# A Mamba-2 layer between two expert layers, one core: weight loads, VectorE's state updates and ScalarE's gated copies in another order

## The reference, cut to what matters

```python
proj = hidden_states @ W_in.T               # z, xBC, dt
xBC = silu(causal_conv(xBC, conv_w, K=4) + conv_b)   # x, B, C
dt = softplus(dt + dt_bias)
Y_diag = einsum('bclhn,bcshn,bhcls,bcshp->bclhp', C_c, B_c, Lmat, x_dt)   # Lmat: decays inside a chunk
states = einsum('bclhn,bhcl,bclhp->bchpn', B_c, decay_states, x_dt)
new = prev * exp(d_k)[..., None, None] + s_k          # the state, chunk after chunk
Y_off = einsum('bclhn,bhcpn,bhcl->bclhp', C_c, prev_states, exp(A_cum))
y = Y_diag + Y_off + D_param * x
g = y * silu(z)
out = (g * rsqrt(mean(g * g) + EPS) * norm_w) @ W_out.T
```

## Time and profile before

| | |
|---|---|
| median of 3 runs | 2531.59 us (2530.6 to 2532.52) |
| profiled execution, its own time | 2530.1 us |
| span of the profiled execution | 2528.3 us |
| TensorE busy | 2290.8 us, 91% of the span |
| VectorE busy | 1742.7 us, 69% |
| GpSimd busy | 1475.2 us, 58% |
| ScalarE busy | 1408.7 us, 56% |

### The profile page before, as it was taken

How to read it: one execution, slowest core, us unless ns; L and a number is a source line. 1 busy time by engine, 2 the same in 40 slices (tenths; PEclk the granted TensorE clock), 3 DMA queues, 4 the chain that set the end, 5 groups by cost and what they waited for, 6 DMA issues and landing times. The chain is left out here.

```text
span 2528.3 us, 44164 instructions
## 1 busy us (share of the span) xinstructions
PE 2290.8 (91%) x11910; PEld 1785.7 (71%) x11910; DVE 1742.7 (69%) x3592; ACT 1408.7 (56%) x2859; POOL 1475.2 (58%) x1306
## 2 busy tenths in 40 slices
PE   4899976999999999999878999999999998489997
PEld 2687755777777777777656777777777776268776
DVE  6532275678787888777867878787878787753225
ACT  3133324677667766776536767677766675323332
POOL 1876341666666666666416666666666665178533
PEclk8999988999999999999889999999999999689998
DMA  8665441333333334333203434443343331166545
GB/s 316 235 184 165 139 135 34 100 88 87 95 103 88 87 95 97 94 87 87 73 10 99 103 88 86 95 102 87 87 95 104 87 87 50 50 224 184 164 151 170
DMA packets 204905, 285.32 MB, mean 113 GB/s; under 512 B 16289, under 2 KB 148459, under 8 KB 204817
## 3 DMA queue, kind: packets, MB, share of 16 engines
q1 hardware_dynamic: 185936, 219.18, 32.4%
q0 software_dynamic: 18880, 65.02, 8.3%
HBM read 225.43 MB, written 58.72 MB: 112 GB/s over the span
## 5 line engine op out<-in xcount | busy, mean ns | idle before, releaser
L1289 POOL TENSOR_TENSOR mamba_mix<-mamba_mix,mamba_scores 128x512 f32<-128x512 f32 x256 | 330.5, 1291 | 278.9 <-ACT mamba_mix L1473 278.9
L1951 PE MATMUL mamba_p_proj<-mamba_xt_lo,mamba_in_hi 128*128 128x512 f32 x1056 | 464.3, 440 | 20.5 <-DVE mamba_bc L1662 11.6
L1952 PE MATMUL mamba_p_proj<-mamba_xt_hi,mamba_in_hi 128*128 128x512 f32 x1056 | 417.1, 395 | 0.0
L1953 PE MATMUL mamba_p_proj<-mamba_xt_hi,mamba_in_lo 128*128 128x512 f32 x1056 | 416.8, 395 | 0.0
L1469 ACT ACTIVATE mamba_mix<-mamba_cum_l,mamba_cum_g 128x128 f32<-128x128 f32 x1024 | 324.5, 390 | 0.0
L1657 DVE SCALAR_TENSOR_TENSOR mamba_xs<-mamba_p_proj,mamba_taps,mamba_xs 128x511 f32<-128x511 f32 (+2 forms) x384 | 285.4, 743 | 40.8 <-ACT mamba_xs L1403 31.7
L1283 POOL TENSOR_TENSOR mamba_xend<-mamba_xdt,mamba_to_end_g 128x512 f32<-128x512 f32 x128 | 160.4, 1253 | 213.7 <-DVE mamba_xdt L1715 213.7
L1688 DVE TENSOR_TENSOR mamba_total<-mamba_p_out,mamba_total 128x512 f32<-128x512 f32 x256 | 176.9, 691 | 149.0 <-PE mamba_p_out L1987 144.4
L643 DVE TENSOR_TENSOR ffn_h<-ffn_p_gu,ffn_sil 128x256 f32<-128x256 f32 x110 | 46.7, 425 | 304.4 <-ACT ffn_sil L532 304.1
L1951 PEld LDWEIGHTS mamba_p_proj<-mamba_xt_lo,mamba_in_hi 128*128 128x128 f32 x1056 | 202.3, 192 | 75.3 <-DVE mamba_bc L1662 12.3
L1953 PEld LDWEIGHTS mamba_p_proj<-mamba_xt_hi,mamba_in_lo 128*128 128x128 f32 x1056 | 200.6, 190 | 45.0
(11 more groups left out here) (334 smaller groups left out, 5465.2 us busy)
## 6 DMA issues: line engine op xcount, KB each, us to landing
mamba_cum_l<-mamba_cum_rows SPq DMA_DIRECT2D x128, 512.0 KB, 6.0
mamba_rise<-mamba_exp_rows SPq DMA_DIRECT2D x256, 128.0 KB, 5.6
ffn_xs<-slots_in SPq DMA_DIRECT2D x78, 256.0 KB, 2.7
slots_out<-ffn_y SPq DMA_DIRECT2D x78, 256.0 KB, 2.3
mamba_raw_x<-in_t SPq DMA_DIRECT2D x34, 512.0 KB, 7.3
mamba_raw_z<-in_t SPq DMA_DIRECT2D x32, 512.0 KB, 8.0
mamba_raw_out<-out_t SPq DMA_DIRECT2D x32, 512.0 KB, 3.7
slots_out<-ffn_xs SPq DMA_DIRECT2D x1, 9984.0 KB, 42.0
```

Source lines behind the costliest of these rows:

```text
L1289: pool.tensor_tensor(mix[:, c % 2, :, :], mix[:, c % 2, :, :], scores[:, b * CPB + c, :].unsqueeze(1).broadcast_to([P, GH, P]), ALU.mult). ...
L1951: pe.matmul(bank, in_hi[:, piece, kk, :], xt_lo[:, kk, c], start=(kk == 0), stop=False)
L1952: pe.matmul(bank, in_hi[:, piece, kk, :], xt_hi[:, kk, c], start=False, stop=False)
L1953: last = pe.matmul(bank, in_lo[:, piece, kk, :], xt_hi[:, kk, c], start=False, stop=(kk == KT - 1))
```

## The change

SyncE: `load_in` for the next group moves ahead of `load_out`, of the decays of half a slot and of their exponentials; the loop now runs from group 2, with group 1's round written ahead of it, and the last three loads follow the loop. ScalarE: `high` of tile 1 moves behind `tap_x` of tile 0. VectorE: `combine` is split in `carry_state` (carried part and state) and `add_skip`; at the start of a slot carry_state(0) stands between the two gating products and add_skip(0) behind them, and combine(1) now precedes add_carry(0). From chunk 2 on `carry_state` has a wait for the sum of two chunks before. No instruction of arithmetic or transfer is added or removed.

```diff
--- before.py
+++ after.py
@@ -1202,20 +1202,29 @@
                     load_cum(k, 0, 0, j, first=True)
                 for j in range(2):
                     load_rise(k, 0, 0, j, first=True)
-                load_cum(k, 0, 1, 0)
-                with sp.Fori(1, G) as gi:
+
+                def round_of(gi, second=False):
                     load_in(gi + (sx + 1), gi * GC + X0, gi * 4 + (sz + 2), gi * GC + Z0)
+                    if not second:
+                        load_out(gi + (k * G - 1), gi - 1)
+                    load_cum(k, gi, -1, 0)
+                    if not second:
+                        load_rise(k, gi, -2, 1)
                     load_cum(k, gi, -1, 1)
                     load_rise(k, gi, -1, 0)
                     load_cum(k, gi, 0, 0)
                     load_rise(k, gi, -1, 1)
                     load_cum(k, gi, 0, 1)
                     load_rise(k, gi, 0, 0)
-                    load_out(gi + k * G, gi)
-                    load_cum(k, gi, 1, 0)
-                    load_rise(k, gi, 0, 1)
+
+                round_of(1, second=True)
+                with sp.Fori(2, G) as gi:
+                    round_of(gi)
                 if k + 1 < batches:
                     load_in(sx + G + 1, B0, sz + 4 * G + 2, DT0, HEADS)
+                load_out(k * G + G - 1, G - 1)
+                load_cum(k, G - 1, 1, 0)
+                load_rise(k, G - 1, 0, 1)
                 load_cum(k, G - 1, 1, 1)
                 for j in range(2):
                     load_rise(k, G - 1, 1, j)
@@ -1511,10 +1520,11 @@
                     for i in range(NB):
                         lns.root(act, k + 1, i)
                 if not first:
-                    for ct in range(CT):
-                        high(U - 1, gp, 1 - b, ct, second)
+                    high(U - 1, gp, 1 - b, 0, second)
                 if not last:
                     tap_x(k, gn, bn, 0, first)
+                if not first:
+                    high(U - 1, gp, 1 - b, 1, second)
                 exponents(k, gi, b, 2)
                 if not first:
                     for ct in range(CT):
@@ -1667,11 +1677,11 @@
                 for i in steps:
                     conv_step(k, gi, b, ct, gi * CT + ct, xs[:, b, ct, :], i)
 
-            def gate(k, gi, b):
+            def gate(k, gi, b, tiles=range(CT)):
 
                 U, V = unit(k, gi, b)
                 dve.wait_ge(s_sum, U * CPB + CPB)
-                for ct in range(CT):
+                for ct in tiles:
                     dve.wait_ge(s_zs, U * CT + ct + 1)
                     dve.tensor_tensor(zs[:, b, ct, :], xs[:, b, ct, :], zs[:, b, ct, :], ALU.mult).then_inc(s_g, 1)
 
@@ -1724,10 +1734,11 @@
                 gn, bn = (gi, 1) if b == 0 else (gi + 1, 0)
                 gp, bp = (gi, 0) if b == 1 else (gi - 1, 1)
 
-                def combine(c):
+                def carry_state(c):
 
                     n = U * CPB + c
-                    cols = slice(c * P, (c + 1) * P)
+                    if c >= 2:
+                        dve.wait_ge(s_sum, n - 1)
                     dve.wait_ge(s_y2, n + 1)
                     if c % 2 == 0:
                         dve.wait_ge(s_rise[c // 2], U * 32 + 32)
@@ -1737,11 +1748,19 @@
                     dve.wait_ge(s_decayed, n + 1)
                     dve.tensor_tensor(state[:, :, :], p_st[:, 0:GC].rearrange("p (h d) -> p h d", h=GH),
                                       decayed[:, :, :], ALU.add).then_inc(s_state, 1)
+
+                def add_skip(c):
+
+                    cols = slice(c * P, (c + 1) * P)
                     for ct in range(CT):
                         done = dve.scalar_tensor_tensor(xs[:, b, ct, cols], xs[:, b, ct, cols],
                                                         skip[:, bass.ds(gi * CT + ct, 1)], p_y[:, c % 2, 0, ct, :],
                                                         ALU.mult, ALU.add)
                     done.then_inc(s_y, 1)
+
+                def combine(c):
+                    carry_state(c)
+                    add_skip(c)
 
                 def add_carry(c):
 
@@ -1778,8 +1797,11 @@
                 if more:
                     layer_norm_of(k + 1)
                 if not first:
-                    gate(k, gp, bp)
-                combine(0)
+                    gate(k, gp, bp, (0,))
+                carry_state(0)
+                if not first:
+                    gate(k, gp, bp, (1,))
+                add_skip(0)
                 if not first:
                     gate_low(U - 1, gp, 1 - b)
                 elif k > 0:
@@ -1787,8 +1809,8 @@
                 next_rows(0, 1)
                 conv(0, (1,))
                 next_stats(0)
+                combine(1)
                 add_carry(0)
-                combine(1)
                 conv(0, (2,))
                 conv(0, (3,))
                 add_carry(1)
```

## The result

The changed kernel is slower: 2569.88 us (median of 4 runs, 2568.17 to 2571.0) against 2531.45 (4 runs of the kernel before), a ratio of 1.0149 with a 95% interval of 1.0136 to 1.0162. The direction was forecast, the size was not: +38 us in place of +15, outside the range of 2518 to 2566. The profiled execution has its own time of 2570.66 us.

The account below looks back on a forecast made before the run. TensorE was taken to bound the groups through its waits between steps. A group: +0.9 us (b = 0) less 0.4 (b = 1), +0.5, times 30 is 15 us, giving 2547 us; range 2518 to 2566.

Parts of the forecast that it names:

- What bounds the kernel: In the groups TensorE bounds, natural pace 4.45 us between recurrences; only its standing still between steps can be won or lost.
- SyncE's part: Next group's x weights issued 13 us earlier, their 1.16 us wait gone; the transfers they are moved past cost nothing.
- ScalarE's part: In b = 0 the second high runs behind tap_x(0); exponents(2) 0.65 us late, recur(2) from 808.31 to 808.94.
- b = 1: Slots with b = 1: state of chunk 0 about 1.3 us earlier, mix(3) 0.65 later; 0.4 us won per slot.
- The step that failed: b = 0, tile 0: low_x(0) holds the last halo piece to 811.0; project_z(0) at 811.15 in place of 809.89.
- r2-r3: Recur(2) to recur(3) in slots with b = 0, forecast to stay at about 5.1 us.
- first rival: In b = 0 low_x(0) goes before tile 0's second halo piece: +0.9 us a group, 28 us, 2559; chance 0.25.
- its worse form: Should mix(3) also precede tile 0's last halo piece, that waits until 812.9: some 1 us a group more, 2585.
- r3-next: Recur(3) of b = 0 to the next slot: forecast 11.6 us, tile 1's last halo piece held by second sum of squares.
- The forecast sum: Per group +0.9 us in b = 0 less 0.4 in b = 1: +0.5, times 30 groups, 15 us.
- The rival that ended on the other side: Holds miss the halo pieces: b = 0 costs +0.1, b = 1 gives 0.4; 9 us faster, 2522; chance 0.15.

Follow-up runs that it names:

- experiment 1: Kernel before with SyncE's part alone: weights issued early, ScalarE's and VectorE's orders as before; ratio to the kernel before 1.0037.
- experiment 6: Kernel before with early weights alone, halo pieces reading their left input from PSUM (left neighbours' values wrong); ratio to the kernel before 0.9892.
- Experiment 4: Changed kernel with GpSimd's low_x(0) moved from in front of mix(3) to right ahead of low_x(1); ratio to the kernel before 1.019.
- experiment 2: Kernel before with ScalarE's part alone: second high behind the first tap, weights late, VectorE's order as before; ratio to the kernel before 1.0104.
- experiment 3: Kernel before with VectorE's part alone: carry_state(0) between the gating products, combine(1) ahead of add_carry(0) in all slots; ratio to the kernel before 1.0015.
- experiment 5: Changed kernel with halo pieces reading their left input from PSUM instead of SBUF (left neighbours' values wrong); ratio to the kernel before 0.9941.
- experiment 7: Kernel before with VectorE's part alone, combine(1) ahead of add_carry(0) only in slots with b = 1, weights late; ratio to the kernel before 0.987.

## Why the prediction was right in its direction and wrong in its size

- *What bounds the kernel* was read rightly: where it waits for nothing TensorE's pace is 4.42 to 4.47 us a step in every run, and all that moved in the groups is waits between its steps.
- *SyncE's part*: as forecast, the weights 12 us earlier (13 said), their wait gone, and the transfers behind them harmless. That an early low_x(0) would fall on the halo pieces was right, and experiments 1 and 6 show it: +0.34 us a group with the pieces held, -0.99 with them free, both against the kernel before.
- *ScalarE's part*: recur(2) late by 0.63 was forecast for b = 0, 0.61 measured; gate_low's wait of 2 us, 2.00 measured.
- *b = 1*: +0.4 won was forecast, 0.54 measured.
- *The step that failed* is the turn between VectorE and GpSimd in b = 0, low_x(0) "runs from about 809.7 to 811.0", and the second halo piece due at about 809.7. I let the piece go first. Both times were right to 0.2 us, their order was not. In the trace low_x(0) starts at 819.85, 10.07 us behind recur(0), and the piece at 820.00, 10.22 behind it, and it is held 0.94 us (1.14 less 0.20). That is the first rival's order, to which I gave 0.25; the last piece then went ahead of mix(3), so its worse form did not come. r2-r3 is 5.58 where the forecast had 5.1.
- *A second term was too small*, in the rival as well. For r3-next I had 11.6 and for the rival's whole slot +1.3; measured 11.82 and +1.61. The forecast had the second sum of squares catch the last piece of tile 1 by its end; it caught the middle one from its start, and held it 1.1 us (1.30 less 0.21). The rival's own times were also added up wrongly: 825.9 less 824.51 is 1.4, not 1.3, and 30 x 0.9 is 27, not 28. Experiment 4 shows that moving one instruction did not free this end: what was freed in tile 0 was held in tile 1.
- *A term was missing*: I multiplied by 30 groups and put nothing on the rest. 10 of the 40 us of the span lie outside the loop groups. The traces tell where 4.3 of them come from: the first groups of the two sequences take 104.4 us together in the kernel before and 108.7 in the changed one, and 104.2, 106.1 and 107.1 in experiments 1, 2 and 3, so ScalarE's part brings 1.7 there, VectorE's 2.7 and SyncE's nothing. The 1.8 us by which the first recurrence is late need not be the change's: in experiment 5, which differs from the changed kernel in the halo pieces alone, it starts at 442.8 us as in the kernel before (442.5). What carries the rest stays open.

The sum with the measured terms is 28 x 1.08 + 10 = 40 us on the span, 1.1 us a group where +0.5 was written. The forecast sum had 15 us; some 16 of the other 25 lie in the loop groups (0.5 a group in r2-r3, 0.2 in r3-next, 0.1 won in b = 1) and 10 outside them. A range whose top case was the first rival's 28 us should have carried those edges too.

The rival that ended on the other side, holds that do not fall on the halo pieces, is what experiment 5 makes of the kernel: its b = 0 is 0.16 us shorter than before (the rival said 0.1 longer), and the ratio of 0.9941 is 15 us, where the rival said 9. So both branches had the right sign, but not the sizes: this one is -0.70 us a group where -0.3 was written. The direction was forecast by either order of the two instructions, 0.15 us apart, so the wrong order did not touch it; it made the loss larger.

## What to carry to other kernels

When a change lets GpSimd start sooner or VectorE later, list which VectorE instructions with two SBUF inputs then meet a GpSimd instruction, down to the smallest: a piece of two columns costs as much as what it runs into. Undo a change of several parts by slot and engine before judging it: here VectorE's part, with its second half kept to the slots with b = 1, was worth -1.3% and the whole was +1.5%. And where two instructions stand within a tenth of a microsecond, price both orders and give neither the name of likeliest; the loop of the changed kernel repeats one order in all 28 groups, that of experiment 3 splits 23 to 5.

## What the runs showed of the hardware

A held halo piece ends with GpSimd's instruction to 0.02 us: 821.14 and 821.12, 826.49 and 826.47 in the changed kernel, 833.31 and 833.29 in experiment 1. Experiments 5 and 6 show that it takes two inputs in SBUF: with the left one in PSUM none of 91 and 92 pieces took more than 215 ns.

Who goes first turns within a few hundredths of a microsecond. In the changed kernel the piece at 825.19 begins 0.01 us before the record of the sum of squares and is held through all of it, while the one at 821.72, 0.19 before mix(3), runs free. Over the traces of the eleven kernels that read the halo from SBUF, all 66 pieces that begin 0.00 to 0.02 us before GpSimd's next record are held, none of the 97 that begin 0.05 to 0.2 before it, and one of the two in between.

It works both ways. mix(3) at 821.91 starts just behind a sum of carried parts that VectorE began at 821.85 (until 822.26), also with both inputs in SBUF, and takes 1.51 us where mix(2) at 817.85 takes 1.28.

A copy with one SBUF input can be held too, which I had not expected. In experiment 7 the copy of 32 columns at the group's turn (before mostly 168 ns) has a median of 1278 ns, since it now begins just behind the start of GpSimd's low part of the output weights: in one group the copy takes from 787.37 to 788.65 us, the low part from 787.31 to 788.61. The copy's line, first before, then in experiment 7:

```profile
L1703 DVE COPY mamba_exp_last_g<-mamba_exp_last x32: 160/168/1290, 434.5 to 2093.7; 128x32 f32 x28, 128x32 f32<-128x32 f32 x4
```

```profile
L1703 DVE COPY mamba_exp_last_g<-mamba_exp_last x32: 169/1278/1292, 435.9 to 2065.0; 128x32 f32 x28, 128x32 f32<-128x32 f32 x4
```

It cost nothing there, since VectorE then still waits 0.86 us for TensorE's transposes. The Trainium skill, "SBUF — State Buffer", section "SBUF: two separate sides", counts VectorE's instructions in a 2-port mode among those that take the shared ports; the trace agrees in so far as this copy ends with an instruction of GpSimd (788.65 and 788.61). No row shows in which mode it runs.

In experiment 3 one and the same execution has both kinds of groups: r3-next is 11.0 us in 5 of them and 11.9 to 12.0 in 23. So the order of one halo piece and low_x(0), turned by a few tenths of a microsecond, is worth 0.9 us in a group.
